# Thirteen graph products: block 24 halved, turns as matmuls, streamed pieces in runs of 8 KB

## The reference, cut to what matters

```python
# third layer: deg, dinv = rsqrt(deg); norm = dinv[row] * edge_weight * dinv[col]
for _ in range(3):
    x = segment_sum(norm[:, None] * x[row], col)      # outs.append(x)
comb = sum(w[l] * outs[l])                            # then divided by its norm
# fourth layer: wn = w * inv_sqrt_out[s] * inv_sqrt_in[d], a self loop of weight 1 added
for _ in range(10):
    h = 0.9 * segment_sum(h[s] * wn[:, None], d) + 0.1 * feat_0
```

## Time and profile before

| | us |
|---|---|
| median of 3 timed runs | 3809.07 (3807.27 to 3817.12) |
| span of the profiled execution | 3796.3 |
| TensorE busy (matmuls) | 2583.5 |
| GpSimd busy | 1839.9 |
| VectorE busy | 1369.5 |
| ScalarE busy | 407.4 |
| DMA traffic | 433.50 MB |

### The profile page before, as it was taken

How to read it: one execution, slowest core, us unless ns; L and a number is a source line. 1 busy time by engine, 2 the same in 40 slices (tenths; PEclk the granted TensorE clock), 3 DMA queues, 4 the chain that set the end, 5 groups by cost and what they waited for, 6 DMA issues and landing times.

```text
span 3796.3 us, 51155 instructions
## 1 busy us (share of the span) xinstructions
PE 2583.5 (68%) x16589; PEld 1756.2 (46%) x16589; DVE 1369.5 (36%) x2536; ACT 407.4 (11%) x940; POOL 1839.9 (48%) x1633
## 2 busy tenths in 40 slices
PE   1565766665666654565656555555669799999997
PEld 1455655555555543554545454555523233333332
DVE  2433434343434324344344444444286311111112
ACT  1111111111111110111111111111100000000000
POOL 0676777676777756777777777777300000000000
PEclk7677767667777756777777777777689899999999
DMA  4211111111111121221212121211069789999997
GB/s 41 40 35 34 35 35 35 35 34 35 24 35 35 35 34 40 44 45 43 45 42 45 44 44 44 44 44 43 18 235 351 278 309 334 345 345 337 343 344 239
DMA packets 387168, 433.50 MB, mean 114 GB/s; under 512 B 184958, under 2 KB 197887, under 8 KB 384046
## 3 DMA queue, kind: packets, MB, share of 16 engines
q1 hardware_dynamic: 324860, 352.87, 28.9%
q0 software_dynamic: 51712, 53.06, 7.7%
q10 hardware_dynamic: 10546, 26.89, 1.9%
HBM read 401.00 MB, written 28.43 MB: 113 GB/s over the span
## 4 chain that ended last, share of the span: by engine, by line
PE 31%; POOL 26%; issue 18%; another core or an unknown queue 12%; DVE 5%; DMA 3%; DVEq 1%; SPq 1%; ACT 1%; POOLq 0%; ACTq 0%
POOL arena L566 26%; PE bank L1353 23%; PE bank L1212 2%; PE bank L1329 1%; DMA arena<-in_edge_weight 1%; PE bank L1224 1%; DMA arena<-d_p,arena 1%; PE bank L1180 1%; DVE arena L654 1%; DVEq L690 1%; DVE arena L696 1%; PE bank L1195 1%; DVE arena L670 0%; DVE arena L671 0%
## 5 line engine op out<-in xcount | busy, mean ns | idle before, releaser
L566 POOL DMA_INDIRECT arena<-d_p,arena x808 | 919.4, 1138 | 396.9 <-issue 364.9
L566 POOL DMA_INDIRECT arena<-d_t,arena x808 | 911.8, 1128 | 393.3 <-issue 352.9
L1353 PE MATMUL bank<-arena 128*64 128x512 f32 (+1 forms) x4550 | 916.1, 543 | 59.2 <-DVE arena L879 33.3
L1224 PE MATMUL bank<-arena 128*128 128x200 f32 x3136 | 758.0, 397 | 79.4 <-issue 77.8
L1224 PEld LDWEIGHTS bank<-arena 128*128 128x128 f32 x3136 | 704.1, 241 | 134.4 <-issue 117.9
L1212 PE MATMUL bank<-arena 128*64 128x47 f32 x3232 | 341.1, 295 | 539.4 <-ACT arena L1028 411.0
L1353 PEld LDWEIGHTS bank<-arena 128*64 128x64 f32 x4550 | 304.3, 136 | 615.3 <-issue 552.8
L1212 PEld LDWEIGHTS bank<-arena 128*64 128x64 f32 x3232 | 313.3, 198 | 594.9 <-issue 326.6
L685 DVE TENSOR_TENSOR arena<-arena 128x1600 f32<-128x1600 f32 x196 | 358.0, 1826 | 6.8
L1213 PE MATMUL bank<-arena 128*64 128x47 f32 x3232 | 344.3, 295 | 3.6 <-issue 3.6
L1180 PE MATMUL bank<-arena 128*96 128x128 f32 x404 | 89.8, 364 | 367.5 <-DVE arena L657 224.0
(11 more groups left out here) (152 smaller groups left out, 1324.8 us busy)
## 6 DMA issues: line engine op xcount, KB each, us to landing
arena<-d_w SPq DMA_DIRECT2D x312, 1024.0 KB, 9.0
d_w<-arena ACTq DMA_DIRECT2D x24, 1024.0 KB
arena<-d_p,arena POOLq DMA_INDIRECT x808
arena<-in_edge_attr SPq DMA_DIRECT2D x101, 128.0 KB
arena<-d_t,arena POOLq DMA_INDIRECT x808
arena<-arena SPq DMA_DIRECT2D x392, 8.0 KB
arena<-in_src SPq DMA_DIRECT2D x202, 4.0 KB
arena<-d_q SPq DMA_DIRECT2D x202, 11.8 KB
```

Of the source, the lines that this page charges most:

```text
L566: g.indirect_dma_start(G[:, b, j, :], None, table, bass.IndirectOffsetOnAxis(ap=idx[:, b, j:j + 1], axis=0)).then_inc(r.g[b], 16)
L1224: last = t.matmul(prod[:, :, WIN * w:WIN * w + WIN], alo[:, b, TPW * w + j, :], outer[:, b, TPW * w + j, :].rearrange("p (c j) -> p c j", ...
L1353: last = t.matmul(banks[t_ % 4][F * (n % 2):F * (n % 2) + F, 0:w_], old[:, n, :], right, start=n < 2, stop=n >= NB - 2)
```

## The change

Three edits.

- **Block 24 halved.** n = 24 becomes two matmuls with the same stationary operand: the first half of the chunk's columns goes to the even group, the second to the odd one. The two groups' results are added behind the turn anyway.
- **Turns as matmuls.** Instead of a transpose by the 128 x 128 identity, the copied values are the stationary operand of a matmul whose moving operand is `fold`, two 64 x 64 identities one above the other. It transposes and adds the two halves at once, so the bank gets 64 columns for each 128 nodes. VectorE's first step (L922, or L924 whose addition moves into a step of its own) and L926 change: in the first three products VectorE reads the bank in its scaling, in the others in the addition of `old`. `fold` is made once, by one VectorE instruction ahead of the products, in the place of `w1ab`; the first load of a piece and the first product wait for it (`NC_X2` 42).
- **Layout of `d_w`.** Partition, part (4 blocks), quarter, block in the part and column. A piece is one run of 8 KB in each partition; a store is four runs of 2 KB.

The general way for unordered edges (`gen_block`) is changed alike; it isn't taken here.

```diff
@@ -57,7 +57,7 @@
-NC_HT, NC_DEG, NC_LEAKY, NC_X2 = 11, 19, 24, 41
+NC_HT, NC_DEG, NC_LEAKY, NC_X2 = 11, 19, 24, 42
...
@@ -114,6 +114,7 @@
+        fold = at(o_w1ab, F)
...
@@ -258,7 +259,7 @@
-        d_w = dram("d_w", [P, NCH * CH // QC, STR, QC])
+        d_w = dram("d_w", [P, NPC, NCH * CH // QC, PIECE * QC])
...
@@ -510,9 +513,9 @@
             def load_piece(j):
                 c, part = j // NPC, j % NPC
-                sp.dma_start(ring[:, j % RING, :].rearrange("p (q e) -> p q e", q=CH // QC),
-                             d_w[:, c * (CH // QC):(c + 1) * (CH // QC), part * PIECE:(part + 1) * PIECE, :]
-                             .rearrange("p q a e -> p q (a e)")).then_inc(s.pc[j % RING], 16)
+                sp.dma_start(ring[:, j % RING, :],
+                             d_w[:, part, c * (CH // QC):(c + 1) * (CH // QC), :]
+                             .rearrange("p q e -> p (q e)")).then_inc(s.pc[j % RING], 16)
             def piece_used(k, j):
...
@@ -863,6 +866,7 @@
+            link2(d.tensor_tensor(fold, ident[:, 0:F], ident[:, F:P], ALU.add))
             assert cnt[0] == NC_X2, cnt[0]
...
@@ -913,31 +917,26 @@
                     lo_ = 4 * c
                     sums(k, c)
                     v.wait_ge(s.out_t, NPOS * k + t_ + 1)
-                    prod = banks[4 + t_ % 4][:, 0:n * P].rearrange("p (a c) -> p a c", c=P)
+                    prod = banks[4 + t_ % 4][:, 0:n * F].rearrange("p (a c) -> p a c", c=F)
                     y = post[:, 0:n, :]
                     if t_ or not isinstance(k, int) or k:
                         v.wait_ge(s.comb_v if steps is step2 else s.xs_v, NPOS * k + t_)
-                    if steps is step2:
-                        d.tensor_copy(y, prod[:, :, 0:F]).then_inc(s.post_v, 1)
-                    else:
-                        d.tensor_tensor(y, prod[:, :, 0:F], old[:, lo_:lo_ + n, :], ALU.add).then_inc(s.post_v, 1)
-                    v.wait_ge(s.post_v, 3 * (NPOS * k + t_) + 1)
-                    d.tensor_tensor(y, prod[:, :, F:P], y, ALU.add).then_inc(s.post_v, 1)
-                    v.wait_ge(s.post_v, 3 * (NPOS * k + t_) + 2)
-                    steps(k, t_, lo_, n, y, old, new)
-
-            def step2(k, t_, lo_, n, y, old, new):
-                d.tensor_tensor(y, y, by_node(dinv, lo_, n), ALU.mult).then_inc(s.post_v, 1)
-                v.wait_ge(s.post_v, 3 * (NPOS * k + t_) + 3)
+                    steps(k, t_, lo_, n, prod, y, old, new)
+
+            def step2(k, t_, lo_, n, prod, y, old, new):
+                d.tensor_tensor(y, prod, by_node(dinv, lo_, n), ALU.mult).then_inc(s.post2_v, 1)
+                v.wait_ge(s.post2_v, NPOS * k + t_ + 1)
                 d.tensor_tensor(new[:, lo_:lo_ + n, :], y, by_node(dinv, lo_, n), ALU.mult).then_inc(s.xs_v, 1)
                 cb = comb[:, lo_:lo_ + n, :]
                 d.scalar_tensor_tensor(cb, y, lwt[:, 13 + k:14 + k], cb, ALU.mult, ALU.add).then_inc(s.comb_v, 1)
             def step3(a):
-                def step(k, t_, lo_, n, y, old, new):
-                    d.tensor_tensor(y, y, by_node(a, lo_, n), ALU.mult).then_inc(s.post_v, 1)
-                    v.wait_ge(s.post_v, 3 * (NPOS * k + t_) + 3)
+                def step(k, t_, lo_, n, prod, y, old, new):
+                    d.tensor_tensor(y, prod, old[:, lo_:lo_ + n, :], ALU.add).then_inc(s.post3_v, 1)
+                    v.wait_ge(s.post3_v, 2 * (NPOS * (k - K2) + t_) + 1)
+                    d.tensor_tensor(y, y, by_node(a, lo_, n), ALU.mult).then_inc(s.post3_v, 1)
+                    v.wait_ge(s.post3_v, 2 * (NPOS * (k - K2) + t_) + 2)
                     d.tensor_tensor(new[:, lo_:lo_ + n, :], y, gb[:, lo_:lo_ + n, :], ALU.add).then_inc(s.xs_v, 1)
                 return step
...
@@ -1045,8 +1044,8 @@
                     return
                 act.wait_ge(s.pair_e[0], 8 * Q + 8 + 1)
                 act.wait_ge(s.pair_e[1], 8 * Q + 8 + 1)
-                act.dma_start(d_w[:, ds(Q, 1), :, :].rearrange("p o a e -> p o (a e)"),
-                              stage[:, q:q + 1, :, :].rearrange("p o a e -> p o (a e)")).then_inc(s.stg[q], 16)
+                act.dma_start(d_w[:, :, ds(Q, 1), :].rearrange("p c o e -> p c (o e)"),
+                              stage[:, q, :, :].rearrange("p (c a) e -> p c (a e)", a=PIECE)).then_inc(s.stg[q], 16)
             def norm(v_sem, v_at, y, tmp_, sc, a_sem):
                 act.wait_ge(v_sem, v_at)
...
@@ -1326,7 +1325,7 @@
                 c = CORDER[slot]
                 for n in range(4 if c < NCH else 1):
                     left = accS[:, slot % 3, P * n:P * n + P] if c < NCH else accL
-                    last = t.transpose(banks[4 + slot % 4][:, P * n:P * n + P], left, ident)
+                    last = t.matmul(banks[4 + slot % 4][:, F * n:F * n + F], left, fold, start=True, stop=True)
                 last.then_inc(s.out_t, 1)
             def product(k, old, first=False, last_=False):
...
@@ -1350,7 +1349,13 @@
                             if (n - RES) % PIECE == 0:
                                 pe.wait_ge(s.pc[piece % RING], 16 * (NPIECE // RING * k + piece // RING + 1))
                             right = ring[:, piece % RING, :].rearrange("p (q a e) -> p a q e", q=CH // QC, e=QC)[:, (n - RES) % PIECE, :, :]
-                        last = t.matmul(banks[t_ % 4][F * (n % 2):F * (n % 2) + F, 0:w_], old[:, n, :], right, start=n < 2, stop=n >= NB - 2)
+                        if n < NB - 1:
+                            last = t.matmul(banks[t_ % 4][F * (n % 2):F * (n % 2) + F, 0:w_], old[:, n, :], right, start=n < 2, stop=False)
+                        else:
+                            for g in range(2):
+                                half = right[:, 2 * g:2 * g + 2, :] if c < NCH else right[:, LASTW // 2 * g:LASTW // 2 * g + LASTW // 2]
+                                last = t.matmul(banks[t_ % 4][F * g:F * g + F, w_ // 2 * g:w_ // 2 * g + w_ // 2], old[:, n, :], half,
+                                                start=False, stop=True)
                         if c < NCH and n < NB - 1 and n >= RES and (n - RES) % PIECE == PIECE - 1:
                             last.then_inc(s.pc_free, 1)
                         if n == (RES - 1 if t_ else TURN_AT) and not (t_ == 0 and first):
```

More of the change, by code:

```diff
@@ L306, in build @@
         s.out_t = sem("out_t")
-        s.post_v = sem("post_v")
+        s.post2_v = sem("post2_v")
+        s.post3_v = sem("post3_v")
         s.xs_v = sem("xs_v")
@@ L390, in blocks @@
             with eng.Fori(0, RES) as n:
-                block_(n, True)
-            with eng.Fori(RES, NB) as n:
-                block_(n, False)
+                block_(n, None, None)
+            with eng.Fori(0, NPC) as part:
+                with eng.Fori(0, PIECE) as a:
+                    block_(PIECE * part + a + RES, part, a)
         def chunks(eng, chunk):
@@ L710, in ordered0, with gen_block @@
                 edge_loop(v, 0, superblock)
-            def gen_block(n, resident):
+            def gen_block(n, part, in_part):
                 steps = 2 * NT + 1
@@ L1065, in gen_block @@
                 for c in range(NCH + 1):
-                    if resident:
+                    if part is None:
                         w_ = CH if c < NCH else LASTW
@@ L1073, in gen_block @@
                         a.activation(W6[:, ds(n - RES, 1), :].rearrange("p o e -> p (o e)"), banks[c][:, 0:LASTW], ACT.Copy).then_inc(s.gen_out, 1)
-                if not resident:
+                if part is not None:
                     act.wait_ge(s.gen_out, (NCH + 1) * (n + 1) + 1)
-                    act.dma_start(d_w[:, :, ds(n - RES, 1), :].rearrange("p q o e -> p q (o e)"),
+                    act.dma_start(d_w[:, ds(part, 1), :, ds(QC * in_part, QC)].rearrange("p o q e -> p (o q) e"),
                                   gen_row.rearrange("p (q e) -> p q e", e=QC)).then_inc(s.gen_st, 16)
```

## The result

The changed kernel is slower: a median of 3833.93 us for 3808.2 us of the kernel before on the same chip, 20 runs each; ratio 1.0066, 95% interval 1.0052 to 1.0080. That is 0.7% and +25.7 us where +8.6 us was forecast: inside the range, on its upper side, three times the forecast sum. The profiled execution went from 3796.3 to 3830.3 us, +34.0.

What follows compares the result with a forecast made beforehand. TensorE's matmuls and turns bound the products, transfers keeping up. Halves -22.4, turns +32.5, VectorE -1.4, pieces -0.3, fold +0.2 gave +8.6 us: 3804.9 profiled, 3817.7 timed (+0.23%), range 3797 to 3836.

Steps and rivals of the forecast that it cites:

- dearer turns: Full turns in the products: upper bound +0.9 us each if no weight load overlapped, where +0.40 was taken.
- the edge loop: Stores now in 2 KB runs beside GpSimd's gathers: taken as 0, rival about -7 or +7 us; 10%.
- milder form of strict order: Chunk to chunk: only the three of four places where block 0 carries a wait lose their gain, 16.8 us, 3834; 7%.
- rival of strict order: Chunk to chunk: block 0 starts only with the second half, four gains gone, +22.4 us on top, 3840; 9%.
- 107 ns quoted in the prediction: Turn passes: the skill's time to load a 128-column stationary operand, said to agree with the trace's 0.113 us spacing.
- -0.05: Full turn: saving in us because the last pass streams 64 columns less, set against +0.45 for four more passes.
- 32.5: All turns of the 13 products: +32.5 us, from 78 x 0.40 + 13 x 0.1, all on the path.
- rival of cheap turns: Turns: weights loaded beside the passes, 0.06 us each, so the 32.5 falls away: -24 us, 3785; 13%.
- 0.91: Behind the third product: VectorE's L922 and L926, 0.91 us with issue, counted in the -1.4 us saved.
- wait for the fourth piece: Start of the first product: TensorE waits 1.0 us for this piece, the one place where piece speed matters.
- One rate within what they tell: Streamed pieces: 386 GB/s in 2 KB runs and 388 in the edge loop's 8 KB stores were judged the same.
- 0.3 of the sum: Pieces in 8 KB runs at the first product's start: -0.3 us taken, bounds -1.0 and +0.4.

Runs made afterwards that it cites:

- halves alone: Kernel before with only block 24 halved; transposes, VectorE's additions and 2 KB runs kept: ratio 0.9927, -27.8 us.
- longer loop: Kernel before with 162 more instructions, waits for a long-come semaphore, in the body of TensorE's loop: ratio 1.0019.
- moved by 193: Changed kernel with 193 more TensorE wait instructions ahead of the first product, loop untouched: ratio 1.0026.

## Why the prediction was right, and where it failed

- **What bounds the kernel.** Right for what it listed: the path in the products is TensorE's. But "a product costs what its matmuls and turns cost TensorE" is where the forecast failed. It left out that TensorE must also have its code. No term stood for it, and 14.9 + 3.3 us of the 34.0 are there. A row that could have warned was on the page: 33 packets of instructions, just the program's 8572 instructions once. So the loop lived in the buffer, and a longer one might not. That the time fell inside the range all the same is luck: its upper side stood there for dearer turns, the edge loop and a milder form of strict order, and a term that none of these describes filled it. The measured 3833.93 even equals that milder form's 3834, which the turns rule out.
- **The halves.** Right: 0.43 saved from chunk to chunk, 0.43 lost in the last chunk (turn to turn 10.21 to 11.08 = 0.43 lost + 0.44 of the turn), block 0 ahead of the second half (3155.68 and 3156.11 us above). With halves alone the product moved by -1.71 us for -1.72. The rival of strict order is out, and so is its milder form: the places with and without a wait on block 0 all gained 0.43 (with halves alone 11.93 became 11.50 us from turn to turn, and 11.60 became 11.17). Strict order would have made a product of the changed kernel 76.1 us; it is 74.75.
- **The turns.** The mechanism is right, 8 passes 0.11 us apart (it is this spacing that agrees with the 107 ns quoted in the prediction; the load's own rows last 0.19 us); the size is 0.44 for 0.40. The step that failed is the "-0.05": the last pass streams 64 columns less, yet the turn grew by the whole of 4 x 0.11. 78 x 0.44 + 13 x 0.1 = 35.6 for 32.5. The rival of cheap turns is out.
- **VectorE and the pieces.** From the last turn to the end it is 20.91 us for 20.90: a longer turn and one instruction less cancel, as counted. Behind the third product the distance from turn to turn scatters between 39.6 and 40.8 us over the profiles, so the 0.91 there can't be seen. The wait for the fourth piece is gone from the first product, which now reads at 427 GB/s for the 386 of the earlier trace rows:

```profile
2791.00:2800.00 9.00, 9.00 (x36) 2.69 (x34) 7.76 (x5) 0.00 (x0) 0.00 (x0) 0.83 1.01 427
```

  "One rate within what they tell" was wrong. What it brought can't be read from this pair: the first chunk, from its first matmul to its turn, took 14.23 us for 14.31, but with the granted clock at 0.50 for its first 5.2 us, for 3.8 before. "Halves alone", in 2 KB runs and with the clock at 0.50 for 5.2 us as well, took 14.88, so the pieces brought some 0.65 us there for the 0.3 of the sum, by one profile each.
- **The test named in advance.** 74.4 to 74.7 us a product: 74.75 came. The forecast asked for the period of a product and would have been content with any one of them; the gaps stand in three products of thirteen, and only the distance from each turn to the next, over all of them, shows them.

## What to carry to other kernels

Before adding instructions to a long loop body, count what one round holds on that engine and how many 16 KB blocks it touches (on TensorE here seven stayed and eight did not), and look at the instruction queue's packets: if they are fewer than rounds times blocks, the loop lives in the buffer, and the addition can end that. When "issue" gaps stand at a jump back, write the loop out or move its start; here 65 idle instructions ahead of it did as much as writing it out. And split a block only where the two groups are uneven: the same edit everywhere gives part of the gain back.

## What the runs showed that was not expected

- Straight code cost nothing visible: with the loop written out 55 blocks came in, one every 25 us through the products, and no turn distance differed by more than 0.01 us from that of the changed kernel outside its gaps and the falls of the clock.
- The price of one jump to code that has gone is not fixed: 4.7 to 5.4 us in the changed kernel (two profiles), 2.0 to 2.1 in the longer loop, 1.5 to 1.8 when moved by 193. The traces show how they differ. The changed kernel stops twice at each of its six jumps, for 1.1 to 1.8 and for 2.7 to 3.2 us, the others once, for 1.3 to 1.8. All 18 stops end 1.3 to 1.7 us behind the end of an instruction packet. By the count above the changed kernel's body begins at most a tenth of a block (25 instructions) ahead of a block's end, and its second stop comes after 11 passes, 22 instructions with their loads; in the other two kernels a fifth of a block or more is left. So the second stop would be the wait for the body's second block. No run tested this by itself.
- At those six jumps TensorE stood 3.9 to 4.6 us in all. Behind four of them the clock fell to 0.50, which cost 1.6 us (3.4 us long) or 3.1 to 3.3 (6.8 long); behind two it did not, the longest stand of 4.6 us among them. After the six stands of 1.3 to 1.8 us it never did.
